# Twelve operations of the first and the last visit move from GpSimd to VectorE, and every place of the layers' order is new

## What is computed

```python
for i in range(NL):                                    # NL = 6
    xn = _adaln(x, noise_emb, n1_w[i], n1_b[i])
    qkv = xn @ qkv_w[i].T
    q, k, v = jnp.split(qkv, 3, axis=-1)
    q = _rope(q.reshape(B, L, H, HD))                  # H = 16 heads of HD = 8
    k = _rope(k.reshape(B, L, H, HD))
    a = _attn(q, k, v, src_mask).reshape(B, L, D) @ so_w[i].T
    x = x + a
    xn = _adaln(x, noise_emb, n2_w[i], n2_b[i])
    q = _rope((xn @ cq_w[i].T).reshape(B, L, H, HD))   # keys, values from a context of 77
    a = _attn(q, k, v, ctx_mask).reshape(B, L, D) @ co_w[i].T
    x = x + a
    xn = _adaln(x, noise_emb, n3_w[i], n3_b[i])
    h = jax.nn.gelu(xn @ f1_w[i].T + f1_b[i], approximate=False)
    x = x + (h @ f2_w[i].T + f2_b[i])
```

## Time and profile before

| | us |
|---|---|
| median of three runs | 2144.84 (2144.10 to 2145.57) |
| the profiled execution | 2146.84 |
| its span in the profile | 2145.0 |
| TensorE busy | 1786.5 (83% of the span) |
| VectorE busy | 1719.4 (80%) |
| ScalarE busy | 1514.2 (71%) |
| GpSimd busy | 1035.6 (48%) |
| the chain that ended last, share by engine | PE 68%, DVE 10%, POOL 5% |

### The profile page before, as it was taken

The page is one execution under the profiler, slowest core; times in us unless marked ns, Lnnn a source line. Parts: engine busy times, 40 slices in busy tenths (PEclk is TensorE's granted clock), DMA queues, the critical chain, the costliest instruction groups (busy, mean ns, idle before and its releaser), DMA issues.

```text
span 2145.0 us, 40593 instructions
## 1 busy us (share of the span) xinstructions
PE 1786.5 (83%) x13134; PEld 767.5 (36%) x13138; DVE 1719.4 (80%) x4125; ACT 1514.2 (71%) x2810; POOL 1035.6 (48%) x1506
## 2 busy tenths in 40 slices
PE   3654277168899999999999999999999999999652
PEld 2332266012333333333343334333343333333222
DVE  7677111579899998999999998999989999998677
ACT  2442021037788998888998888988888998888553
POOL 2554531734445564545654555554545555534432
PEclk9676589569999999999999999999999999999775
DMA  3001122232413334334333235233344333431100
GB/s 107 5 0 40 37 88 88 58 99 61 113 38 95 86 82 98 75 82 98 97 86 92 67 82 125 78 78 93 68 107 99 81 76 85 96 95 43 31 2 20
DMA packets 139788, 158.35 MB, mean 74 GB/s; under 512 B 39855, under 2 KB 107431, under 8 KB 137255
## 3 DMA queue, kind: packets, MB, share of 16 engines
q1 hardware_dynamic: 137535, 151.54, 28.5%
q0 software_dynamic: 2048, 4.20, 0.7%
HBM read 84.90 MB, written 68.38 MB: 71 GB/s over the span
## 4 chain that ended last, share of the span: by engine, by line
PE 68%; DVE 10%; POOL 5%; issue 3%; ACT 2%; DMA 1%; SPq 0%; POOLq 0%; DVEq 0%; ACTq 0%
PE ps L1379 16%; PE ps L1332 9%; PE ps L1343 9%; PE ps L1390 4%; PE ps L1481 4%; DVE smax L1900 4%; PE ps L1491 4%; PE ps L1455 3%; PE ps L1431 2%; PE ps L1415 2%; PE ps L1354 2%; PE ps L604 2%; PE ps L1448 2%; PE ps L614 2%; PE ps L1366 1%
## 5 line engine op out<-in xcount | busy, mean ns | idle before, releaser
L1608 ACT ACTIVATE big<-ps 128x512 f32<-128x512 f32 x1920 | 1006.7, 612 | 147.1 <-PE ps L1343 140.0
L1900 DVE TENSOR_REDUCE smax<-ps 128x1 f32<-128x512 f32 x1536 | 962.0, 682 | 88.9 <-PE ps L1332 82.0
L1379 PE MATMUL ps<-big,vaug 128*32 128x512 f32 x3072 | 411.2, 608 | 0.0
L1332 PE MATMUL ps<-k,q 49*128 49x512 bf16 x1536 | 291.2, 389 | 22.4 <-DVE smax L1900 16.7
L1343 PE MATMUL ps<-q,k 52*128 52x512 bf16 x1536 | 291.9, 385 | 8.5 <-DVE smax L1900 2.5
L1811 POOL CAST mparts<-smax 128x16 bf16<-128x16 f32 x96 | 19.2, 200 | 351.8 <-DVE smax L1900 351.8
L1908 DVE TENSOR_REDUCE maxima<-ps 128x4 f32<-128x308 f32 x384 | 155.7, 469 | 19.2 <-PE ps L1366 14.9
L1332 PEld LDWEIGHTS ps<-k,q 49*128 49x128 bf16 x1536 | 75.2, 94 | 251.6 <-DVE smax L1900 130.6
L1343 PEld LDWEIGHTS ps<-q,k 52*128 52x128 bf16 x1536 | 76.4, 94 | 204.3 <-issue 55.6
L1797 POOL TENSOR_TENSOR rot<-rot,cs 128x512 f32<-128x512 f32 x72 | 92.3, 1281 | 97.4 <-DVE rot L1919 97.3
L1802 POOL TENSOR_TENSOR hat<-rot,rparts 128x512 f32<-128x512 f32 x72 | 83.4, 1160 | 58.8 <-ACT rparts L1656 58.6
(11 more groups left out here) (312 smaller groups left out, 2938.9 us busy)
## 6 DMA issues: line engine op xcount, KB each, us to landing
k<-scratch_keys SPq DMA_DIRECT2D x192, 112.0 KB
q<-scratch_queries SPq DMA_DIRECT2D x192, 96.0 KB
cq<-scratch_cross_queries SPq DMA_DIRECT2D x48, 384.0 KB, 5.8
scratch_keys<-rparts SPq DMA_DIRECT2D x48, 192.0 KB, 2.9
scratch_queries<-rparts SPq DMA_DIRECT2D x48, 192.0 KB
scratch_cross_queries<-rparts SPq DMA_DIRECT2D x48, 192.0 KB
scratch_keys<-rparts SPq DMA_DIRECT2D x48, 128.0 KB, 2.4
scratch_queries<-rparts SPq DMA_DIRECT2D x48, 128.0 KB
```

What stands on the lines that cost most here:

```text
L1332: last = nc.tensor.matmul(out[u], m.q6[rows, v % 2, 2 * g + pr, qt * P:(qt + 1) * P], m.k6[rows, v % 2, 2 * g + pr, :], start=True, stop=True)
L1379: last = nc.tensor.matmul(m.ps[32 * j:32 * j + 32, pv_bank, :], of_head(m.vaug, v % 2 * TB + kt, g, j), of_quad("self", q)[:, j, :], start ...
L1608: nc.scalar.activation(of_quad(kind, p // 2)[:, p % 2 * 2 + u, :], bank("exp" if kind == "self" else "cross exp", p, u), ACT.Exp, scale=sc ...
L1900: nc.vector.tensor_reduce(m.smax[:, n % 2, qt, u, pr:pr + 1], bank("max", i, u), AX.X, ALU.max).then_inc(s_read["self"], 1)
```

## The change

Twelve operations have an entry in a new table `MOVED_PLACES` and go to VectorE: for visit 0 the normalisation `next`, and for its query and key the second half of the rotation, the remainder and the third part; for visit 23 the normalisations `cross` and `ff` (with the addition of the feed-forward's bias to the state), and the same three steps of the cross query. GpSimd still makes the root for these normalisations. `in_turn` adds a wait where neighbouring visits are on different engines, so that a semaphore's counts come in order. All other numbers of the tables are new too; the diff shows a few of them and the code in full. No instruction is added or dropped besides.

```diff
--- before.py
+++ after.py
     "next": (
-        -326701, 13478, 107286, 156386, 248181, 311894, 375078, 438526, 501822, 565533, 628388, 691875, 755264, 818998, 881914, 945302,
-        1008547, 1072693, 1136093, 1199560, 1263148, 1326885, 1389897, 1453255),
+        -329653, 27004, 108927, 158080, 249775, 313275, 376329, 439467, 503221, 566357, 630277, 693807, 757053, 820266, 883468, 946865,
+        1010656, 1074011, 1137685, 1201075, 1264038, 1327280, 1391300, 1454421),
...
-    "POOL norm cross": (86666,),
+    "POOL norm cross": (88750,),
...
-    "SP store key 0": (-48600,),
+    "SP store key 0": (-43098,),
...
-    "SP weights context": -8467,
+    "SP weights context": -96524,
...
-    "POOL block bias": (1806408, 1853836, 1912885, 2152244),
+    "POOL block bias": (1645236, 1833846, 2038291, 2093808),
...
-    "DVE block find": (1555694, 1682470, 1834651, 2193099),
+    "DVE block find": (1563877, 1678605, 1766799, 2103128),
...
-    "DVE block begin": (1446859, 1507626, 1618100, 1715462),
-    "POOL begin fetch": (-1080434, -844532, -683233, -390259),
-    "DVE begin combine": (-829654, -537343, -325033, -254062),
-    "POOL begin root": (-729965, -418590, -50221, -39779),
-    "DVE begin state": (-674089, -115634, -48981, -17639),
+    "DVE block begin": (1446640, 1509123, 1608027, 1690931),
+    "POOL begin fetch": (-849514, -804490, -676598, -394564),
+    "DVE begin combine": (-767269, -506169, -211540, -173654),
+    "POOL begin root": (-716212, -315014, -180336, -83207),
+    "DVE begin state": (-488600, -172216, -153154, -9695),
+}
+MOVED_PLACES = {
+    "DVE less cross": {23: 1555585},
+    "DVE less key": {0: -382805},
+    "DVE less query": {0: -379422},
+    "DVE normal cross": {23: 1540644},
+    "DVE normal ff": {23: 1669807},
+    "DVE normal next": {0: -392969},
+    "DVE rotate cross": {23: 1552240},
+    "DVE rotate key": {0: -385524},
+    "DVE rotate query": {0: -383299},
+    "DVE third cross": {23: 1558536},
+    "DVE third key": {0: -375469},
+    "DVE third query": {0: -369656},
 }
...
@@ -1012,11 +1026,20 @@
         self.of[name] = dict(enumerate(places))
         self.when[name] = {at: i for i, at in self.of[name].items()}
 
+    def move(self, name, places):
+        self.of[name], self.when[name] = dict(places), {at: i for i, at in places.items()}
+        other = "POOL" + name[3:]
+        for i, at in places.items():
+            if other in self.of:
+                del self.when[other][self.of[other][i]]
+                self.of[other][i] = at
+
     def at(self, name, i):
         return self.of[name][i]
 
     def due(self, name, at):
-        return [self.when[name][at]] if at in self.when[name] else []
+        places = self.when.get(name, {})
+        return [places[at]] if at in places else []
 
     def moments(self, engine):
         return sorted({at for name, places in self.when.items() if name.split()[0] == engine for at in places})
@@ -1077,7 +1100,16 @@
         pl.put_once(name, BLOCK_PLACES[name])
     for name in BEGIN_PLACES:
         pl.put_once(name, BEGIN_PLACES[name])
+    for name in MOVED_PLACES:
+        pl.move(name, MOVED_PLACES[name])
     at, due = pl.at, pl.due
+
+    def on_dve(work, kind, i):
+        return i in MOVED_PLACES.get(f"DVE {work} {kind}", ())
+
+    def in_turn(engine, work, kind, i, done):
+        if i and on_dve(work, kind, i) != on_dve(work, kind, i - 1):
+            engine.wait_ge(done, i)
 
     qb = {n: sem(f"block_{n}") for n in (
         "weights", "rows", "hidden_rows", "weight_sums", "sums_ready", "ternary", "dve", "pool", "moments_first", "moments_second", "moments_hidden",
@@ -1774,10 +1806,13 @@
                 st, b, chain = m.sts[kind], v % B, chains[kind]
                 pool.wait_ge(t_stats[kind], v + 1)
                 before = row_before[kind, v]
-                if before is not None:
+                if before is not None and not on_dve("normal", kind, v):
                     pool.wait_ge(t_turned[before[0]], before[1] + 1)
                 chain.link(nc.gpsimd.tensor_scalar(st.var[:], st.mv[:, :, 1], LN_EPS, None, ALU.add))
                 chain.link(nc.gpsimd.tensor_tensor(st.rstd[:], st.var[:], m.minus_half[:], ALU.pow))
+                if on_dve("normal", kind, v):
+                    return
+                in_turn(pool, "normal", kind, v, t_hat[kind])
                 for t in range(TB):
                     last = normalise(nc.gpsimd, m.rows[:, row[kind, v]], m.state[:, b * TB:(b + 1) * TB, :], t, st)
                 last.then_inc(t_hat[kind], 1)
@@ -1788,6 +1823,7 @@
                     nc.gpsimd.tensor_tensor(rows, rows, m.f2b[:].unsqueeze(1).to_broadcast([P, TB, D]), ALU.add).then_inc(biased, 1)
 
             def rotate(kind, i):
+                in_turn(pool, "rotate", kind, i, x_rot[kind])
                 pool.wait_ge(x_read[kind], i + 1)
                 x = turned(kind, i)
                 if kind == "context":
@@ -1798,11 +1834,13 @@
                 nc.gpsimd.tensor_tensor(x[:, 0, :], x[:, 0, :], x[:, 1, :], ALU.add).then_inc(x_rot[kind], 1)
 
             def less_first(kind, i):
+                in_turn(pool, "less", kind, i, x_low[kind])
                 pool.wait_ge(x_hi[kind], i + 1)
                 nc.gpsimd.tensor_tensor(rest_of(kind, i), turned(kind, i)[:, 0, :], parts_of(kind, i)[:, 0, :],
                                         ALU.subtract).then_inc(x_low[kind], 1)
 
             def third_part(kind, i):
+                in_turn(pool, "third", kind, i, x_lo[kind])
                 pool.wait_ge(x_mid[kind], i + 1)
                 parts = parts_of(kind, i)
                 nc.gpsimd.tensor_tensor(parts[:, 2, :], rest_of(kind, i), parts[:, 1, :], ALU.subtract).then_inc(x_lo[kind], 1)
@@ -2049,6 +2087,42 @@
                 nc.vector.tensor_scalar(m.tern[0][:], m.tw[0], -1.0, None, ALU.max)
                 nc.vector.tensor_scalar(m.tern[1][:], m.tw[1], -1.0, None, ALU.max).then_inc(qb["ternary"], 1)
 
+            def normal_rows(kind, v):
+                st, b = m.sts[kind], v % B
+                dve.wait_ge(t_pool[kind], 2 * (v + 1))
+                in_turn(dve, "normal", kind, v, t_hat[kind])
+                before = row_before[kind, v]
+                if before is not None:
+                    dve.wait_ge(t_turned[before[0]], before[1] + 1)
+                rows = m.state[:, b * TB:(b + 1) * TB, :]
+                for t in range(TB):
+                    last = normalise(nc.vector, m.rows[:, row[kind, v]], rows, t, st)
+                last.then_inc(t_hat[kind], 1)
+                if kind == "ff":
+                    dve.wait_ge(w_sem["ff"], 48 * (v // B + 1))
+                    dve.wait_ge(t_hat["ff"], v + 1)
+                    in_turn(dve, "normal", kind, v, biased)
+                    nc.vector.tensor_tensor(rows, rows, m.f2b[:].unsqueeze(1).to_broadcast([P, TB, D]), ALU.add).then_inc(biased, 1)
+
+            def rotate(kind, i):
+                in_turn(dve, "rotate", kind, i, x_rot[kind])
+                dve.wait_ge(x_read[kind], i + 1)
+                x = turned(kind, i)
+                b_chain.link(nc.vector.tensor_tensor(x[:, 1, :], x[:, 1, :], m.cs[:, 1, :], ALU.mult))
+                nc.vector.tensor_tensor(x[:, 0, :], x[:, 0, :], x[:, 1, :], ALU.add).then_inc(x_rot[kind], 1)
+
+            def less_first(kind, i):
+                in_turn(dve, "less", kind, i, x_low[kind])
+                dve.wait_ge(x_hi[kind], i + 1)
+                nc.vector.tensor_tensor(rest_of(kind, i), turned(kind, i)[:, 0, :], parts_of(kind, i)[:, 0, :],
+                                        ALU.subtract).then_inc(x_low[kind], 1)
+
+            def third_part(kind, i):
+                in_turn(dve, "third", kind, i, x_lo[kind])
+                dve.wait_ge(x_mid[kind], i + 1)
+                parts = parts_of(kind, i)
+                nc.vector.tensor_tensor(parts[:, 2, :], rest_of(kind, i), parts[:, 1, :], ALU.subtract).then_inc(x_lo[kind], 1)
+
             def begin_block(b):
                 dve.wait_ge(f_added, VISITS - B + b + 1)
                 rows = of_batch(m.x, b)
@@ -2115,6 +2189,10 @@
                 last.then_inc(qb["done"], 1)
 
             for now in pl.moments("DVE"):
+                for work, do in (("normal", normal_rows), ("rotate", rotate), ("less", less_first), ("third", third_part)):
+                    for kind in rounds if work != "normal" else TURNS:
+                        for i in due(f"DVE {work} {kind}", now):
+                            do(kind, i)
                 for b in due("DVE begin combine", now):
                     combine(b)
                 for b in due("DVE begin state", now):
```

282 lines of the change are left out of this document (141 added, 141 removed), and 12 rows, old and new, of the table OFFSETS.

## The result

The changed kernel's median was 2115.82 us (2114.97 to 2122.26 in four runs) against 2144.47 us of the kernel before: a ratio of 0.9873, 95% interval 0.9853 to 0.9894, so 28.7 us faster. Two later measurements of the same kernel gave 2113.95 against 2144.67 (0.9858, 0.9843 to 0.9873) and 2113.12 against 2145.62 (0.9862, 0.9843 to 0.9880). The forecast was 2125.5 with a range from 2118: the sign was right and so were the two ends as the main places, but the gain was half as large again and 4 us of it lie in the full stretch, where none was forecast. In two of the 13 executions of these three measurements the mean granted clock was 0.914 and the time 2122.2 and 2122.3 us, against 0.921 to 0.924 and 2112.3 to 2117.7 in the others; neither was profiled, so where these 8 us lie is open. The profiled execution took 2116.31 us (span 2114.6), against 2146.84 (2145.0).

The account below looks back on a forecast made before the run. The prediction took TensorE to bound the kernel for 21 visits from about 586 us. From 2144.8 us, -10.5 + 0.6 - 3.2 - 3.9 - 2.3 = -19.3 gave 2125.5 us, range 2118 to 2138.

Parts of the forecast that it names:

- Bound and places: TensorE bounds the 21 visits from about 586 us; the change was expected to gain at head and tail.
- Head, first and second link: Visit 0's earlier root, normalisation and rotation on VectorE: first maximum 15.2 us earlier, of which 10.5 last at the 17th.
- the work that stands before every later addition is the same in both orders: Behind the 17th maximum: claimed that the head's 10.5 us gain is passed on to all later additions.
- Full stretch: The visits where TensorE is full: the new order costs 0.6 us, bounds -4 and +6 for waits.
- 858 such steps from bf16 to f32 now and 865 then: TensorE's order in the full stretch: each such step costs 0.08 us more, giving +0.6 us.
- Tail, visits 22 and 23: Visit 23's cross normalisation on VectorE and a less disturbed visit 22 normalisation on GpSimd: 3.2 us gained, bounds 0 and 6.0.
- Visit 23's feed-forward: At the tail, a shorter normalisation saves 2.0 us and the last addition's queue wait 1.9: 3.9 us gained.
- Last block: Bias additions and quantisation save 1.3 us and batch 3's moments come 1.0 earlier: 2.3 us gained, bounds 0 and 3.0.
- Rival (c): Slower: TensorE waits once a visit for a bank VectorE hasn't read; 1.2 us each, 2150.7 us; chance 0.07.
- The rule against the change: At the head, VectorE's two-port mode blocks GpSimd's last gathers: they end 6.5 us later, sum -18.7 instead of -19.3.

Follow-up runs that it names:

- up_late: The kernel before with the first of a visit's four up products moved behind the exponent's and maximum's pair, next to the second; 2139.43 us (0.9967).
- after_up: The changed kernel with the four up products of a visit together; 2136.66 us (0.9964).
- after_down: The changed kernel with only the third quarter of the down products moved next to the fourth; 2134.86 us (0.9949).
- moves_tail: The kernel before, every place as it was, with only visit 23's operations moved to VectorE; 2140.50 us (0.9975).
- moves_norm: The kernel before with only visit 0's first normalisation, four instructions, moved to VectorE; 2142.53 us (0.9989).
- head_unmoved: The changed kernel with its places, but visit 0's seven operations stay on GpSimd; 2126.20 us (0.9918).
- ff22_moved: The changed kernel with visit 22's feed-forward normalisation also moved to VectorE; 2113.02 us against 2144.44 (0.9857).

## Why the prediction was right and wrong

- **Bound and places**: right in the main. The full stretch is TensorE's, and most of the gain sits at the two ends; but 4.0 to 4.2 us sit in the full stretch.
- **Head, first and second link** (-10.5): right mechanism, too small by 3.1. From the gather on, the first maximum came 0.9 us earlier than forecast (422.48 + 2.83 = 425.31 against 426.2): the eight operations took 5.49 us (405.74 to 411.23), not 5.9, and the recorded sum is 0.4 too long in itself, since 422.3 with two states of 1.1 and moments of 1.3 makes 425.8. The list between first and 17th took 24.75 us and not 25.9: each shuffle with its product put in 1.2 us and not 1.35, TensorE's waits 0.6 and not 1.6. Behind the 17th another 0.7 us came until addition 0. Rounding is the rest. That moves and places alone give 3.3 and 3.5 us and together 13.6 did not spoil the forecast, which priced them together; but whoever had priced one of them by it would have been wrong. The step "the work that stands before every later addition is the same in both orders" left out the clock, 0.94 instead of 0.89 from the 17th maximum to addition 0.
- **Full stretch** (+0.6): wrong, and with 4.7 and 4.8 us in the later two profiles the largest miss (2.4 in the first, which lost 2.5 us there). The step that failed is "858 such steps from bf16 to f32 now and 865 then" at 0.08. The price of the way back, 0.20 for ending a 32-bit group, was left out, and so was a change from one 32-bit kind to another, though the profile of before has both. Between additions 1 and 63 the traces hold 870 groups of 32-bit products of one kind in before and 851 in after, while the steps from bf16 to 32 bit grew from 763 to 768; 19 groups at 0.20 are 3.8 us. up_late showed that the up pair alone makes it.
- **Tail, visits 22 and 23** (-3.2): right; additions 67 to 69 gained 2.8 us in the first profile and 3.6 and 3.7 in the later ones.
- **Visit 23's feed-forward** (-3.9): right, 3.95 (28.06 - 24.11). **Last block** (-2.3): right, 2.3. The tail's excess over 9.4 lies in the step from addition 69 to 70 (0.8 us in each profile) and in 0.5 us ahead of addition 67.
- **Ahead of the first gather**: no term at all, where 1.1 to 3.2 us came; see the last section.
- **Rival (c)**, a wait for a maxima bank once a visit: the new order does have it in nearly every visit (L1364 <- smax, 20 times), but for 0.3 us and not 1.2. after_up and after_down show what a wait once a visit can cost, there for banks that ScalarE's exponentials and `on_rows` read: 16.5 and 12.5 us in the rows above.
- **The rule against the change**: two gathers took 1.39 and 1.03 us and a root 1.52, so the last gather ended about half a microsecond late, and not 6.5; the Trainium skill's full block (SBUF — State Buffer, Who interferes with whom) did not appear behind these operations. The same section gives such a mode to tensor_scalar but not to tensor_tensor, so by it only the normalisation, 1.1 of the 6.5 us, could have blocked in that way.

So the range missed because four terms were off to the same side: ahead of the first gather, head, full stretch and tail by 2.8, 3.2, 2.4 and 1.0 us in the first profile and by 3.2, 3.3, 4.7 and 2.1 in the third. The bounds of the full stretch, -4 and +6, were set for waits alone, and it came out at the very end of them by another way.

## What to carry to other kernels

When an operation and the order move together, find each chain that ends at the first instruction of the next stage (its data, and the queue of the engine that takes it), since lifting one of two gives no more than the distance to the other (here 4.1 and 7.3 us alone, 16.1 together at the first maximum). Then follow the gain to where TensorE is full: 2.4 us at the first maximum were nothing at addition 0, where its clock was lower. In a stretch that repeats, price every change of kind on TensorE, to a 32-bit group and back from it, and count groups rather than steps of one sort; but group only by delaying work that nobody awaits, since a product put ahead of an awaited pair costs more than the change. Take a difference between two profiles only after checking it against the medians or a second profile, since each of the first two here held one loss of 1.7 to 2.5 us beside a dip of the clock.

## What was not expected of the hardware

**The clock ahead of the gathers.** The instructions of every engine are the same for the first 365 us in all twenty profiles, yet they fall in two patterns. In the seven with all of visit 0's operations on GpSimd, the 32 products of the logits took 6.83 or 6.84 us; in the thirteen with at least one on VectorE, 3.85 to 3.94, and their first gather came 0.6 to 3.2 us earlier than in before, in the seven it lay between -0.35 and +0.19. Rows of before and after:

```profile
216.43 6.84 PE L628 MATMUL ps<-wg,xnT 128*128 128x8 f32 x32
```

```profile
216.43 3.92 PE L628 MATMUL ps<-wg,xnT 128*128 128x8 f32 x32
```

The parting starts near 41 us, with the engines' work ahead of it alike: the same two products take 1.02 us in moves_tail and 1.92 in the second profile of after.

```profile
41.13 1.02 PE L320 MATMUL ps<-xnT,w 128*128 128x512 f32 x2
```

```profile
41.49 1.92 PE L320 MATMUL ps<-xnT,w 128*128 128x512 f32 x2
```

The clock had risen ahead of the first pair and not yet ahead of the second: the traces record the first rise to the higher level (2.4 GHz) at 40.9 us in moves_tail and at 43.9 in the second profile of after. In the seven it lies between 40.8 and 41.4 us, in the thirteen between 41.7 and 44.4, and in the three profiles of the changed kernel alone at 42.1, 43.9 and 41.7. The first gather follows this rise by 326.6 to 326.8 us in the seven and by 322.8 to 323.1 in the thirteen. So within a pattern the start of the first gather is set by when the clock first rose, and the differences of up to 2.1 us between the three profiles of after come with it.

From 50 to 60 us the granted clock is 0.72 to 0.75 in the seven and 0.77 to 0.90 in the thirteen, from 210 to 220 us 0.50 against 0.58 to 0.67. moves_norm, with one operation of the seven, has the early gather, and head_unmoved, with the whole new order but none of visit 0's moves, the late one, so in these profiles it goes with visit 0's operations on VectorE and not with the order. That the one causes the other is not shown: why code that runs 350 us later should matter was not found, and of the executions without a profile it is not known which pattern they had. These 1 to 3 us are in the difference between the profiles, and no profile of before alone would have told them.

**Who pays beside whom.** Eight multiplies of VectorE took 2.3 us alone and 8.75 beside GpSimd's rotation, whose own operations took 1.26 to 1.31 us there as elsewhere: the delay fell on VectorE. In the last block GpSimd paid as well: its scaling took 3.24 us beside VectorE's additions of 128x2048 in ff22_moved, and 1.27 in another batch (1971.96 above), while one of those additions took 3.23 instead of 2.28.
